# Two cross attention stages on one core: another order of rounds for the wide stage, and the statistics of one chunk moved behind its maxima in the latent stage

## The reference, cut to what matters

```python
# latent: 4 heads of 64, keys and queries normed to unit root mean square
q, k, v = split_heads(ln @ Wq.T), ...            # k, v from the context and from the latents
attn = softmax(where(mask, qn @ kn.T, -max))
out = (attn @ v) @ Wo.T + bo
...
# wide: 16 heads of 16
scores = einsum('bhid,bhjd->bhij', x @ Wq, context @ Wk) * scale
attn = softmax(where(mask, scores, -max))
out = einsum('bhij,bhjd->bhid', attn, context @ Wv) @ Wo
```

## Time and profile before

| | us |
|---|---|
| median of 3 runs (lowest, highest) | 3732.11 (3730.59, 3732.14) |
| the profiled execution | 3735.25 |
| its span in the trace | 3733.4 |
| PE, DVE, ACT, POOL busy | 3021.3, 2553.5, 1931.4, 788.9 |
| one round of the latent stage | 36.4 |
| one round of the wide stage | 41.2 |

### The profile page before, as it was taken

The page is one execution under the profiler, slowest core; times in us unless marked ns, Lnnn a source line. Parts: engine busy times, 40 slices in busy tenths (PEclk is TensorE's granted clock), DMA queues, the critical chain, the costliest instruction groups (busy, mean ns, idle before and its releaser), DMA issues. The chain is left out here.

```text
span 3733.4 us, 103978 instructions
## 1 busy us (share of the span) xinstructions
PE 3021.3 (81%) x36990; PEld 2577.0 (69%) x36990; DVE 2553.5 (68%) x7510; ACT 1931.4 (52%) x4178; POOL 788.9 (21%) x849
## 2 busy tenths in 40 slices
PE   3349999999999995666539999999999999944398
PEld 3338888888888884445427878888788888733266
DVE  5558888888888882676647777777777777646311
ACT  1136666666766662333215666666666666622121
POOL 0222333233332320000031221222122212100123
PEclk8669999999999996777659999999999999966599
DMA  2132323323232312000011111111111111031471
GB/s 63 47 90 79 84 80 82 84 79 83 79 85 81 84 36 70 12 23 23 12 45 38 41 42 41 40 44 40 40 41 44 40 40 43 18 121 56 153 206 23
DMA packets 246318, 226.61 MB, mean 61 GB/s; under 512 B 80068, under 2 KB 239077, under 8 KB 245680
## 3 DMA queue, kind: packets, MB, share of 16 engines
q1 hardware_dynamic: 232480, 208.39, 20.3%
q0 software_dynamic: 13328, 11.56, 1.0%
HBM read 187.00 MB, written 33.42 MB: 59 GB/s over the span
## 5 line engine op out<-in xcount | busy, mean ns | idle before, releaser
L1867 ACT ACTIVATE xb_P<-xb_sc 124x1024 f32<-124x1024 f32 (+1 forms) x416 | 405.6, 1023 | 426.8 <-PE xb_sc L1959 426.8
L2029 DVE CUSTOM_DVE_ANT_0 xb_junk<-xb_ring,xb_mbias 128x372 bf16<-128x372 f32 (+2 forms) x1024 | 526.0, 571 | 99.3 <-PE xb_ring L1936 95.0
L1936 PE MATMUL xb_ring<-xb_khi,xb_qhi 32*128 32x372 f32 (+2 forms) x1024 | 404.0, 439 | 45.7 <-DVE xb_kf L2014 16.8
L879 PE MATMUL xa_acc<-xa_raw,xa_P 124*128 124x193 f32 x1664 | 315.6, 330 | 7.2 <-ACT xa_P L754 7.2
L1959 PE MATMUL xb_sc<-xb_qs,xb_kf 32*124 32x128 f32 x6656 | 317.3, 271 | 0.0
L2014 DVE COPY xb_kf<-xb_ring 128x372 f32<-128x372 f32 (+2 forms) x256 | 138.6, 571 | 244.3 <-ACT xb_khi L1831 239.2
L1907 PE MATMUL xb_ring<-xb_xst,xb_whi 128*128 128x372 f32 (+2 forms) x768 | 262.8, 369 | 43.8 <-DVE xb_xst L2008 38.0
L1907 PE MATMUL xb_ring<-xb_whi,xb_xst 128*124 128x256 f32 (+1 forms) x1248 | 284.4, 291 | 3.1 <-DVE xb_maxes L2029 0.6
L1936 PEld LDWEIGHTS xb_ring<-xb_khi,xb_qhi 32*128 32x128 f32 x1024 | 180.7, 183 | 152.9 <-DVE xb_maxes L2029 57.7
L1959 PEld LDWEIGHTS xb_sc<-xb_qs,xb_kf 32*124 32x124 f32 x6656 | 282.7, 182 | 0.0
L879 PEld LDWEIGHTS xa_acc<-xa_raw,xa_P 124*128 124x128 f32 x1664 | 266.4, 189 | 18.5 <-ACT xa_P L754 12.4
(11 more groups left out here) (433 smaller groups left out, 7783.1 us busy)
## 6 DMA issues: line engine op xcount, KB each, us to landing
xa_raw<-in_ctx SPq DMA_DIRECT2D x64, 279.0 KB
ex_w<-in_W SPq DMA_DIRECT2D x16, 1024.0 KB, 11.5
xa_raw<-in_ctx SPq DMA_DIRECT2D x32, 372.0 KB
xa_xTr<-in_ctxT SPq DMA_DIRECT2D x64, 186.0 KB
xb_raw<-in_ctxT SPq DMA_DIRECT2D x64, 186.0 KB, 2.5
xa_xTr<-in_ctxT SPq DMA_DIRECT2D x32, 248.0 KB, 2.8
xb_raw<-in_ctxT SPq DMA_DIRECT2D x32, 248.0 KB
xa_mask<-in_mask SPq DMA_DIRECT2D x32, 200.1 KB
```

The source lines that it names most:

```text
L879: i = nc.tensor.matmul(acc[:, o, :], w, raw[0:KEYS, t3, t, :], start=t == 0 and o == 0, stop=t == NKT - 1, skip_group_check=True)
L1867: nc.scalar.activation(P[0:w, pbuf(t, p), :].rearrange("p (r n) -> p r n", r=4), sc[0:w, :, half], ACT.Exp).then_inc(sem("exped"), 1)
L1936: i = nc.tensor.matmul(bank[:, 0:w], qhi[r, p, o, 128 * s:128 * s + 128], khi[r, p, o, k0:k0 + w], start=True, stop=True)
L2029: v.tensor_tensor_reduce(out=junk[:, k, 0:w], in0=ring[f % 3][:, 0:w], in1=mbias[:, p, k0:k0 + w], scale=1.0, scalar=-3.0e38, op0=ALU.add, ...
```

## The change

In the latent stage three steps move. `Y` 3 of batch n + 2 leaves its place ahead of `A` 3 and stands behind `X` 2; `mred` moves ahead of `X` 2; `YA` 3 and `YB` 3 move behind `K` 0 and `RS` 0. The order of PE, POOL and SP stays as it was.

In the wide stage the whole list is new. The two `B` of a pair stand side by side; `A` is no longer packed between them three at a time, but taken singly or on either side of a pair; single `PV` steps, `V` and `K` stand between. `Q2` moves ahead and `F2` far back, `S` 3 to the front of the round, `S` 2 of n + 2 to its end, `Q1` ahead of `B` 12. `FILLS` gets the batch offset of each fill by a rule (`behind`) instead of by constants, since `F1` and `M` now stand elsewhere.

```diff
-                  ("B", 5), ("PV", 4), ("A", 2), ("Yn", 2), ("STn", 1), ("Xn", 1), ("KT", 3), ("YAn", 2), ("SEn", 1), ("YBn", 2), ("Yn", 3),
-                  ("B", 6), ("PV", 5), ("A", 3), ("AL", 0), ("STn", 2), ("Xn", 2), ("mred", 0), ("YAn", 3), ("SEn", 2), ("YBn", 3),
-                  ("Kn", 0), ("RSn", 0), ("PV", 6), ("M", 0), ("F0", 0)]
+                  ("B", 5), ("PV", 4), ("A", 2), ("Yn", 2), ("STn", 1), ("Xn", 1), ("KT", 3), ("YAn", 2), ("SEn", 1), ("YBn", 2),
+                  ("B", 6), ("PV", 5), ("A", 3), ("AL", 0), ("mred", 0), ("STn", 2), ("Xn", 2), ("Yn", 3), ("SEn", 2),
+                  ("Kn", 0), ("RSn", 0), ("YAn", 3), ("YBn", 3), ("PV", 6), ("M", 0), ("F0", 0)]
...
-        ROUNDS = [("Ln", 0), ("Ln", 1), ("A", 0), ("B", 0), ("A", 1), ("B", 1), ("A", 2), ("X", 2), ("K", 1), ("F1", 0), ("PV", 0),
-                  ("A", 3), ("B", 2), ("A", 4), ("B", 3), ("S", 3), ("K", 2), ("V0", 0), ("F2", 0), ("Q2", 0), ("PV", 1), ("PV", 2),
-                  ("A", 5), ("B", 4), ("A", 6), ("B", 5), ("A", 7), ("X", 3), ("V1", 0), ("V0", 1), ("PV", 3), ("PV", 4),
-                  ("A", 8), ("B", 6), ("A", 9), ("B", 7), ("A", 10), ("Sn", 0), ("K", 3), ("V1", 1), ("Qn", 0), ("PV", 5), ("PV", 6),
-                  ("A", 11), ("B", 8), ("A", 12), ("B", 9), ("Xn", 0), ("Sn", 1), ("V0", 2), ("V1", 2), ("PV", 7), ("PV", 8),
-                  ("A", 13), ("B", 10), ("A", 14), ("B", 11), ("A", 15), ("Sn", 2), ("V0", 3), ("V1", 3), ("mred", 0), ("PV", 9), ("PV", 10),
-                  ("B", 12), ("Q1n", 0), ("Xn", 1), ("Kn", 0), ("M", 0), ("PV", 11), ("PV", 12), ("F0", 0)]
+        ROUNDS = [("Ln", 0), ("Ln", 1), ("S", 3), ("A", 0), ("B", 0), ("A", 1), ("B", 1), ("A", 2), ("X", 2), ("V0", 0), ("A", 3),
+                  ("PV", 0), ("K", 1), ("F1", 0), ("Q2", 0), ("B", 2), ("B", 3), ("A", 4), ("X", 3), ("K", 2), ("PV", 1), ("V1", 0),
+                  ("A", 5), ("B", 4), ("B", 5), ("A", 6), ("PV", 2), ("A", 7), ("PV", 3), ("Qn", 0), ("PV", 4), ("A", 8), ("V0", 1),
+                  ("A", 9), ("B", 6), ("B", 7), ("A", 10), ("PV", 5), ("V1", 1), ("K", 3), ("PV", 6), ("A", 11), ("Sn", 0), ("B", 8),
+                  ("B", 9), ("A", 12), ("PV", 7), ("V0", 2), ("Sn", 1), ("V1", 2), ("B", 10), ("Xn", 0), ("A", 13), ("B", 11), ("PV", 8),
+                  ("F2", 0), ("A", 14), ("V0", 3), ("Xn", 1), ("Q1n", 0), ("A", 15), ("mred", 0), ("B", 12), ("PV", 9), ("PV", 10),
+                  ("V1", 3), ("Kn", 0), ("M", 0), ("PV", 11), ("PV", 12), ("Sn", 2), ("F0", 0)]
...
+        def behind(kind, n):
+
+            return (-2 if kind in OF_B else -3 if kind in ("F1", "F2") else 0 if kind in OF_NEXT else -1) + (n < turn)
```

More of the change, by code:

```diff
@@ L1623, in wide_cross_attention @@
         turn = ROUNDS.index(("Kn", 0))
-        for kind, c in ROUNDS[turn:] + ROUNDS[:turn]:
+        def behind(kind, n):
+            return (-2 if kind in OF_B else -3 if kind in ("F1", "F2") else 0 if kind in OF_NEXT else -1) + (n < turn)
+        for at in range(turn, turn + len(ROUNDS)):
+            kind, c = ROUNDS[at % len(ROUNDS)]
+            d = behind(kind, at % len(ROUNDS))
             if kind in ("Kn", "K"):
-                FILLS += [(("K", c, o), "kf", 8, 2 * c + o, 0) for o in range(2)]
+                FILLS += [(("K", c, o), "kf", 8, 2 * c + o, d) for o in range(2)]
             elif kind == "V0":
-                FILLS += [(("V", c, 0), "val", 8, 2 * c, 0)]
+                FILLS += [(("V", c, 0), "val", 8, 2 * c, d)]
             elif kind == "V1":
-                FILLS += [(("V", c, 1), "val", 8, 2 * c + 1, 0)]
+                FILLS += [(("V", c, 1), "val", 8, 2 * c + 1, d)]
             elif kind == "A":
-                FILLS += [((kind, c, o), "maxed", 32, 2 * c + o, 0) for o in range(2)]
+                FILLS += [((kind, c, o), "maxed", 32, 2 * c + o, d) for o in range(2)]
             elif kind == "M":
-                FILLS += [((kind, c, 0), "augq", 1, 0, -1)]
+                FILLS += [((kind, c, 0), "augq", 1, 0, d)]
             elif kind == "F1":
-                FILLS += [((kind, c, 0), "lden", 1, 0, -2)]
+                FILLS += [((kind, c, 0), "lden", 1, 0, d)]
         while len(FILLS) % len(ring):
```

## The result

The changed kernel takes 3622.34 us (median of four runs, 3617.7 to 3623.21), the kernel before 3732.05 us in the runs beside it (3730.59 to 3732.14): a ratio of 0.970, 95% interval 0.969 to 0.972. It is faster by 110 us; the prediction was 3617 us, range 3582 to 3672.

The account below looks back on a forecast made before the run. PE was taken to bound both stages, with DVE pacing its runs of `A`. From 3735.3 us, 28 (latent) and 87 (wide) came off, giving 3620, or 3617 us as median; range 3582 to 3672.

Parts of the forecast that it names:

- PE runs at DVE's pace within the packed `A`: Wide stage: DVE's maxima pace runs of `A`; 6.8 us of stalls a round, 7.3 with the wait of `A` 3.
- Wide, 2.8 us a round: Wide-stage round falls from 41.2 to 38.4 us, so 2.8 less; 87 us over 31 rounds.
- The term for what stays: Wide stage: stalls left a round, 1.4 us at `A` 0 to `A` 2, 1.5 elsewhere (bounds 0 and 3.5).
- Changes of shape, 1.6 us a round: Wide stage on PE: 30 changes of array shape a round instead of 21 cost 1.6 us more.
- third rival: Wide stage: nine extra shape changes cost 0.8 us each, kernel slower, 3791 us; chance 0.04.
- Latent, 0.95 us a round: Latent stage: `K` 0 starts 1.2 us earlier, less 0.25; 28 us (15 to 42) over 30 rounds.
- `YB` 3's 0.25 us: Latent stage on DVE: `YB` 3 now ahead of `F0` and `R` 0 costs 0.25 us a round.
- cover of 1.32 us for `Y` 3: Latent stage: DVE's idle 1.32 us ahead of L960 is just enough for `Y` 3's 1.25 us.
- second rival: Latent stage: `Y` 3 costs as much in its new place, only the wide stage gains; 3645 us, chance 0.07.
- Sum: Whole kernel: 3735.3 - 28 - 87 = 3620 us, 3617 us as the median of runs.
- first rival: Wide stage: half of the stalls just move, a round falls by 1.2 us; kernel 3667 us, chance 0.13.
- `X` 0 took what was said beside an idle POOL: Wide stage: first part of `X` 0 on DVE takes 0.67 us instead of 1.94, away from POOL's mask tile.

Follow-up runs that it names:

- runs 2 and 6: 2: new wide list with the latent list of before, 3657.6 us; 6: changed kernel, `A` 4, 6, 10, 12 between the `B` of their pair again, 3669.5 us.
- run 9: Changed kernel with `A` 0 to `A` 2 taken apart as in run 7, but `X` 2 on DVE behind `A` 3: 3614.7 us.
- run 8: Changed kernel with `V1` 3 between `PV` 9 and 10, `M` between `PV` 11 and 12, four more shape changes a round: 3633.8 us.
- run 1: Kernel before with only the latent list changed, wide list as before: 3692.9 us.
- run 11: Changed kernel with `YA` 3 and `YB` 3 at the very end of the latent round, behind `F0`: 3624.7 us.
- run 7: Changed kernel with `A` 0 to `A` 2 taken apart, `X` 2 ahead of the maxima of `A` 2: 3678.7 us.

## Why the prediction was right, point by point

- **PE runs at DVE's pace within the packed `A`.** The stalls were there and went away (runs 2 and 6). The reason held for the old list: from its first maximum on, DVE works there without a pause, and PE goes at its steps of 0.46 us. What the prediction did not have is the second limit close behind it, the trip of a bank: halved maxima took only 83 us instead of 140 to 200 from the old list, since the trip fell only from 1.21 to 1.03 us.
- **Wide, 2.8 us a round.** Measured 2.46. The end, 38.4, is nearly what was measured (38.50 in the round shown, 38.60 in the mean), 0.2 us too low by the mean, 6 us in all; the start was too high, since the one round of the earlier trace rows lay above the mean of 41.06. That error is 0.17 us a round, 5 us in all; a mean over many rounds would have spared it. The term for what stays (1.4 for `A` 0 to `A` 2, 1.5 for leftovers) is not shown by its parts: `A` 7 is 0.28 us late, and halved maxima take 1.5 us more out of a changed round, but taking `A` 0 to `A` 2 apart saved only 0.2 (run 9). That the sum of a round comes out so close does not show each term.
- **Changes of shape, 1.6 us a round.** Those that run 8 could price, between columns and the whole array, cost 0.09 to 0.13 us against the 0.16 taken, so for them the term was too large. `A` to `PV` and `PV` to `V` or `K`, which no row showed, take 0.35 us and 0.57 us from start to start. Both are as priced from the engine that has to empty: 0.36 for a last `A`, and for a `PV` its own 0.44 us (two of them take 1.01) with the 0.13 of the way out. The third rival is out, since a round fell by 2.46 us. By the Trainium skill (TensorEngine Tiling (Array Packing), Key Properties) the engine drains at a change of mode, and run 8 shows changes that cost a tenth of a microsecond each, not a matmul.
- **The turn of the loop** was in no step. The round with it is 8.5 us longer than the others, before 4.5; since run 1 has 7.2 with the old wide list, what the change has to do with it is not shown.
- **Latent, 0.95 us a round.** Measured 1.27 in the round shown, 37.7 / 30 = 1.26 by run 1. The step that was mis-sized is `YB` 3's 0.25 us: it costs nothing (run 11), and `KT` 0 waits 0.5 us as before, not 0.75. The cover of 1.32 us for `Y` 3 was just enough, as worked out: 0.16 us is left. The second rival is out.
- **Sum.** 37.7 + 72.9 = 110.6 us, predicted 115. The latent term was 10 us too small and the wide one 14 too large: that the end, 3617 against 3622 us, is nearer than either term is luck. Of the 14 us, 5 and 6 are the start and the end of a round as said above; the last 3 are not traced. The first rival (wide stage half of it, 37 us) is out by 36 us. Neither of the two errors alone would have left the range.

`X` 0 took what was said beside an idle POOL; its first part after, on DVE:

```profile
2318.65 0.67 DVE L2013 TENSOR_TENSOR xb_xst<-xb_raw,xb_xst 64x496 fp32r<-64x496 f32 x1
```

That is 0.67 us instead of 1.94. No run tested what it is worth in the end.

## What to carry to other kernels

Where a few banks go around between two engines, measure the whole trip of a bank (here 1.2 us from a matmul to the next into the same bank) and put that much other work between two users; speeding up the consumer helps only until the trip is the limit. A busy share of 96% may hide such stalls, so read the distance between starts. When steps are moved in one list for all engines, look at what the move puts ahead of what on every engine: `X` 2 on DVE made of a sound order on PE a kernel 56 us slower than the changed one.

## What the hardware showed that I had not expected

An idle stretch of PE of only 0.92 us was followed, 0.7 to 2.0 us later, by 3.4 us at half the clock, in 24 of 29 rounds of run 7. The length of the wait alone does not decide it: in the other five rounds the clock stayed at 1.00 behind the same wait, and in the latent stage of the kernel before PE waits 1.2 us in nearly every round, as in the earlier trace rows, and the clock stays at 1.00. Here is the stretch of 10 us around that wait of the earlier trace rows:

```profile
816.00:826.00 10.00, 8.82 (x69) 8.01 (x68) 8.29 (x31) 6.97 (x19) 3.81 (x6) 1.00 0.33 83
```

What else decides was not tried and stays open. At the turn of the loop the clock falls too, behind a wait of 5.1 us. That wait is 3.5 us in the kernel before and 5.4 in run 1, which has the same wide list, so it isn't the new list that makes it longer; the cause stays open.
